# A two-layer decoder on one core: work of the opening regrouped between GpSimd, ScalarE and VectorE

## The chip, the cores and the metric

The kernel runs on one core of a Trainium2 chip. The metric is the device time of one execution in microseconds (us). A core has five engines with a queue each: TensorE (PE, matrix products; its weight loads are listed as PEld), VectorE (DVE), ScalarE (ACT), GpSimd (POOL) and SyncE (SP, which here only issues transfers). Each works through its own list in order and waits on semaphores. Transfers (DMA) can be issued by SP, ACT and POOL; an issuing engine is held for the issue, not for the transfer.

## The reference, cut to what matters

Two decoder layers over `x` of 8 batches x 256 tokens x 128 features. The opening of the kernel, which the change is in, works on the first of six residual blocks:

```python
def _L0_attn_ref(x, W_qkv, b_qkv, W_out, b_out):     # 16 heads of 8 columns
    qkv = x @ W_qkv.T + b_qkv
    q, k, v = jnp.split(qkv, 3, axis=-1)
    ...
    scores = jnp.einsum('bhqd,bhkd->bhqk', q, k) / jnp.sqrt(jnp.float32(HEAD_DIM))
    att = jax.nn.softmax(scores, axis=-1)
    out = jnp.einsum('bhqk,bhkd->bhqd', att, v)
    ...
    return out @ W_out.T + b_out
...
x = x + _L0_attn_ref(_layernorm(x, axis=-1), ...)
x = x + _L0_xattn_ref(_layernorm(x, axis=-1), ctx_1024, ...)   # needs K and V of ctx_1024
x = x + _L0_ffn_ref(_layernorm(x, axis=-1), ...)
x = x + _L1_attn_ref(_layernorm(x, axis=-1), ...)
x = x + _L1_xattn_ref(_layernorm(x, axis=-1), ctx_1024, ctx_1024, ...)
x = x + _L1_ffn_ref(_layernorm(x, axis=-1), ...)
```

## The kernel before, in words

Every engine has its list written out by hand; nothing is scheduled automatically. The first block runs batch by batch in steps `i` = -3 to 7 (`steps_of`), each with 16 places `h`, one for each head. In step `i`, PE computes the real scores of batch `i` (`scores`, line 1324) and, beside them, the scores of batch `i + 1` that are only used to find each row's maximum (`scores_for_max`, line 1333). DVE reduces these to row maxima (`row_max`, 954), ACT takes the exponentials (`exps`, 658), PE forms the weighted sums (1370). Steps -3, -2 and -1 are the opening: layer norms, projections and stacks are prepared for the first batches, and in step -1 the row maxima of batch 0 are found. Step 0 is the first full one.

How a batch gets ready for its scores: DVE takes statistics (`ln_stats`, 927 and 930), POOL turns them into a reciprocal deviation (`rstd_step_`, 511 and 513), DVE applies the norm (`ln_apply`, 938), PE transposes and projects (1272, 1280, 1284), ACT copies queries and keys to `qkf` (681). Then `split` (407 to 412) breaks the float32 values of `qkf` into three bfloat16 parts in `parts`, so that six products of parts (`TERMS`) give nearly float32 scores. It runs on DVE for batches 0 and 1 (`FIRST` keeps them off POOL) and on POOL for the others. Last, DMAs copy the parts into `stack` in the order of the six terms, six loads for the queries and six for the keys of a batch. SP issues them (`load_stack`, 470), except for the six key loads of batch 0, which POOL issues (`load_first_keys`, 533). `stack` has three slots (batch number mod 3). POOL clears each once with a memset (`clear_stack`, 504), and SP then writes rows of ones into it (`fill_stack`, 435). PE waits for a batch's stack in `wait_stacked`.

Keys and values of the context for the second block come from eight projections, `kv_project` (1296, 1298), copied by ACT (686, 688). `KV_AT` says in which step and at which place they stand, and PE waits for all of their copies before step 0. `BUSY` says at which places PE multiplies the identity with itself with no use of the result (`stay_busy`, 1265), to have something to do. `prepare_v_aug` (908, 910) are DVE memsets of the buffer for the values, two slots at a time.

Of the kernel before, what the change touches and what calls it, by code (L numbers as in the profile page):

```python
# [67 lines left out]
KV_AT = {-2: (15, 15, 15), -1: (1, 4, 7, 10, 13)}  # L68

FIRST = (0, 1, B, B + 1, B + 2)  # L70
# [15 lines left out]
BUSY = {(-3, 0): 10, (-3, 5): 2, (-3, 9): 4, (-2, 0): 2, (-2, 5): 2, (-2, 9): 3, (-1, 4): 3, (-1, 10): 3,  # L86
# [3 lines left out]
def build(nc, t):  # L90

    ctx = ExitStack()
    with ctx:
# [183 lines left out]
        def wait_stacked(eng, n):  # L277

            if n == 0:
                eng.wait_ge(first_keys, STACKED // 2)  # L280
            eng.wait_ge(stacked[n % 3], STACKED * (n // 3 + 1) - (STACKED // 2 if n % 3 == 0 else 0))
# [134 lines left out]
        def _(sp):  # L416
# [22 lines left out]
            for s3 in range(3):  # L439
                fill_stack(s3)  # L440
# [31 lines left out]
            for lo in MANY:  # L472
                for i in range(lo - 3, lo + B):
                    if has(i + 3, lo):
                        load_stack(i + 3)
                    if lo == 0:
                        load_for_later(i)
# [11 lines left out]
        def _(pool):  # L489
# [39 lines left out]
            def load_first_keys():  # L529

                pool.wait_ge(parts_ready, 1)
                for r, (jq, jk) in enumerate(TERMS):
                    pool.dma_start(stack[r::DH, 0, 1], parts[:, 0, 1, jk, :]).then_inc(first_keys, 16)
# [72 lines left out]
            for lo in MANY:  # L606
# [12 lines left out]
                for n in range(lo, lo + B):  # L619
                    if n == 0:  # L620
                        rstd_step_(0)
                        rstd_step_(1)
                        clear_stack(1)
                        clear_stack(2)
                        load_first_keys()
                    elif 2 <= n < B or n == B + AHEAD_C:
                        rstd_step_(item(n))
# [24 lines left out]
        def _(act):  # L652
# [72 lines left out]
            def v_copy_ahead(m):  # L725
# [3 lines left out]
                               pv_ps[1][:, 0, :].rearrange("p (h d) -> p h d", d=DH), ACT.Copy).then_inc(v_ready, 1)  # L729

# [60 lines left out]
            for lo in MANY:  # L791
# [33 lines left out]
                for i in steps_of(lo):  # L825
                    x = prepared(i, lo)
                    for h in range(H):
# [23 lines left out]
                        if h == 15 and x is not None and has(i + 3, lo):  # L851
                            v_copy(i + 3)
                        if h == 0 and lo == B and has(i - 3, lo):
# [50 lines left out]
        def _(dve):  # L904
# [174 lines left out]
            for lo in MANY:  # L1079
# [29 lines left out]
                for i in steps_of(lo):  # L1109
                    x = prepared(i, lo)  # L1110
                    for h in range(H):
# [4 lines left out]
                        if (lo == 0 and h == 0 or (i, h) == (B, 1)) and ln is not None and ln != 1:  # L1116
                            ln_stats(ln)
                            if ln == 0:
                                ln_stats(1)
                        if has(i + 1, lo):  # L1120
# [7 lines left out]
                        if h == 3 and i == -3:  # L1128
                            prepare_v_aug(slice(2, 4), 2)
# [5 lines left out]
                        if (i, h) == (-2, 9):  # L1135
                            split(dve, 1)
# [625 lines left out]
```

## Time and profile before

| | |
|---|---|
| time, median of 3 runs | 397.46 us (396.42 to 400.72) |
| time of the profiled execution | 399.4 us |
| its span in the trace | 397.6 us |
| PE busy | 354.7 us (89% of the span) |
| PE weight loads | 210.5 us (53%) |
| DVE busy | 314.7 us (79%) |
| ACT busy | 265.6 us (67%) |
| POOL busy | 160.4 us (40%) |
| granted PE clock, mean | 0.985 of 2.4 GHz |

A profile shows one execution. A timeline row gives start, duration, engine, line, operation and tiles, with the idle time before it and what ended it in brackets. The chain of waits leads back from the last instruction, at each step to what released it. "Granted clock" is the share of its full 2.4 GHz that PE was given in a stretch. All times in the rows are us from the start of the span.

### The profile page before, as it was taken

How to read it: one execution, taken by the hardware profiler on the slowest of the kernel's cores; microseconds unless marked ns; L12 is line 12 of the kernel's file. 1: busy time of each engine (PE TensorE's matmuls, PEld its weight loads, DVE VectorE, ACT ScalarE, POOL GpSimd, SP SyncE). 2: the span in 40 equal slices, each digit the busy share in tenths (PEclk: the TensorE clock that was granted, in tenths of full speed). 3: DMA queues.
4: the chain of work that ended last, by engine and by line, in shares of the span. 5: the costliest groups of instructions: out<-in, count | busy, mean ns of one | idle time of the engine just before them, and what ended most of it. 6: DMA issues, size and time to landing. Idle time of an engine off the chain costs nothing.

```text
span 397.6 us, 9590 instructions
## 1 busy us (share of the span) xinstructions
PE 354.7 (89%) x3246; PEld 210.5 (53%) x3246; DVE 314.7 (79%) x874; ACT 265.6 (67%) x594; POOL 160.4 (40%) x267
## 2 busy tenths in 40 slices
PE   6889999999999889987887969999889899989994
PEld 6765444444444468775266834444444444447564
DVE  7778889989998277976367667898988997479995
ACT  3436888888878757767306666887777887765751
POOL 8425653565200023445006274157677422370001
PEclk9999999999999999999899898999999999999999
DMA  7442243224330000002000311311311300000003
GB/s 221 124 109 53 77 115 81 54 51 115 91 134 2 2 0 3 0 2 66 14 2 3 80 42 40 83 43 41 81 35 49 82 2 3 2 1 2 1 2 106
DMA packets 35830, 20.00 MB, mean 50 GB/s; under 512 B 4150, under 2 KB 34790, under 8 KB 35782
## 3 DMA queue, kind: packets, MB, share of 16 engines
q1 hardware_dynamic: 34982, 17.81, 16.9%
q10 hardware_dynamic: 608, 1.18, 0.8%
q8 instruction: 27, 0.44, 0.5%
q0 software_dynamic: 192, 0.39, 0.4%
q14 instruction: 21, 0.17, 0.1%
HBM read 5.58 MB, written 1.05 MB: 17 GB/s over the span
## 4 chain that ended last, share of the span: by engine, by line
PE 64%; DVE 13%; issue 6%; ACT 6%; POOL 5%; DMA 3%; SPq 2%; ACTq 0%; POOLq 0%; DVEq 0%
PE pv_ps L1370 15%; PE s_ps L1324 14%; PE s_ps L1427 4%; DVE negmax_sb L954 3%; PE prep_ps L1280 3%; PE s_ps L1333 3%; ACT probT_sb L658 3%; PE s_ps L1663 3%; PE out_ps L1482 2%; DVE xn_sb L938 2%; PE s_ps L1450 2%; PE prep_ps L1284 2%; PE s_ps L1510 2%; PE s_ps L1500 2%; PE out_ps L1401 2%
## 5 line engine op out<-in xcount | busy, mean ns | idle before, releaser
L954 DVE TENSOR_REDUCE negmax_sb<-s_ps 128x2 bf16<-128x512 f32 x256 | 163.9, 691 | 33.9 <-PE s_ps L1333 33.2
L658 ACT ACTIVATE probT_sb<-s_ps 128x512 f32<-128x512 f32 x256 | 143.3, 596 | 32.3 <-PE s_ps L1324 29.1
L1324 PE MATMUL s_ps<-stack_sb 63*128 63x256 bf16 x512 | 89.9, 273 | 11.1 <-ACT probT_sb L658 4.7
L1333 PE MATMUL s_ps<-stack_sb 62*128 62x256 bf16 x512 | 87.1, 274 | 6.0 <-DMA stack_sb<-parts_sb 4.6
L1370 PE MATMUL pv_ps<-probT_sb,v_aug_sb 128*32 128x256 f32 x1024 | 68.8, 386 | 0.5 <-ACT probT_sb L658 0.5
L1324 PEld LDWEIGHTS s_ps<-stack_sb 63*128 63x128 bf16 x512 | 30.8, 94 | 67.3 <-ACT probT_sb L658 38.2
L511 POOL TENSOR_SCALAR rstd_sb<-mv_sb 128x2 f32<-128x2 f32 x32 | 7.2, 225 | 100.5 <-DVE mv_sb L930 100.1
L1370 PEld LDWEIGHTS pv_ps<-probT_sb,v_aug_sb 128*32 128x32 f32 x1024 | 26.8, 109 | 25.9 <-issue 13.2
L1333 PEld LDWEIGHTS s_ps<-stack_sb 62*128 62x128 bf16 x512 | 29.6, 94 | 12.2 <-DMA stack_sb<-parts_sb 5.6
L681 ACT ACTIVATE qkf_sb<-prep_ps,b_qkv_sb 128x256 f32<-128x256 f32 x56 | 23.9, 470 | 13.7 <-PE prep_ps L1284 13.7
L938 DVE TENSOR_SCALAR xn_sb<-x_all_sb,mv_sb,rstd_sb 128x128 f32<-128x128 f32 x64 | 23.9, 465 | 3.8 <-POOL rstd_sb L513 3.6
L1192 DVE SCALAR_TENSOR_TENSOR late_sb<-late_sb,level_sb,k_inv_sb 8x256 f32<-8x256 f32 x49 | 23.2, 474 | 1.8
L513 POOL TENSOR_TENSOR rstd_sb<-rstd_sb,minus_half_sb 128x2 f32<-128x2 f32 x32 | 22.9, 716 | 2.7
L1280 PE MATMUL prep_ps<-xnT_sb,w_att_sb 128*128 128x256 f32 x64 | 21.9, 425 | 0.1
L407 POOL CAST parts_sb<-qkf_sb 128x512 bf16<-128x512 f32 x14 | 8.5, 609 | 29.9 <-ACT qkf_sb L681 29.9
L1427 PE MATMUL s_ps<-xrT_sb,d_w_sb 128*128 128x512 f32 x40 | 19.5, 611 | 0.8 <-ACT late_sb L746 0.8
L521 POOL TENSOR_TENSOR x_all_sb<-x_all_sb,b_vo_sb 128x256 f32<-128x256 f32 x16 | 11.5, 728 | 18.6 <-DVE xn_sb L938 18.5
L746 ACT ACTIVATE late_sb<-s_ps,d_b_sb 128x512 f32<-128x512 f32 x20 | 13.4, 686 | 6.1 <-PE s_ps L1427 6.1
L1007 DVE SCALAR_TENSOR_TENSOR x_all_sb<-out_ps,den_inv_sb,x_all_sb 128x128 f32<-128x128 f32 x32 | 9.8, 346 | 9.1 <-PE out_ps L1482 9.0
L412 POOL TENSOR_TENSOR parts_sb<-rest_sb,parts_sb 128x512 bf16<-128x512 f32 x14 | 16.2, 1160 | 1.1
L409 POOL TENSOR_TENSOR rest_sb<-qkf_sb,parts_sb 128x512 f32<-128x512 f32 x14 | 16.2, 1156 | 1.1
L410 POOL TENSOR_TENSOR parts_sb<-qkf_sb,parts_sb 128x512 bf16<-128x512 f32 x14 | 16.2, 1157 | 0.0
(206 smaller groups left out, 648.5 us busy)
## 6 DMA issues: line engine op xcount, KB each, us to landing
stack_sb<-parts_sb SPq DMA_DIRECT2D x186, 64.0 KB, 2.1
x_all_sb<-x SPq DMA_DIRECT2D x4, 256.0 KB, 3.3
ctxT_sb<-ctxT ACTq DMA_DIRECT2D x2, 512.0 KB, 6.6
f_w_sb<-f_w SPq DMA_DIRECT2D x2, 512.0 KB, 4.3
out<-x_all_sb SPq DMA_DIRECT2D x4, 256.0 KB, 2.4
d_w_sb<-d_w SPq DMA_DIRECT2D x2, 320.0 KB, 3.6
w_att_sb<-w_att SPq DMA_DIRECT2D x2, 256.0 KB, 4.0
stack_sb<-maxrow_sb ACTq DMA_DIRECT2D x32, 4.0 KB
```

Source lines behind the costliest of these rows:

```text
L409: eng.tensor_tensor(rest[:, :, :], qkf[:, w], parts[:, u, :, 0, :], ALU.subtract).then_inc(rest_ready, 1)
L513: pool.tensor_tensor(rstd[:, u, :], rstd[:, u, :], minus_half[:, 0:NT], ALU.pow).then_inc(rstd_ready, 1)
L658: act.activation(probT[:, c % 8], s2_ps[c % 2][:, :, :], ACT.Exp, scale=DH ** -0.5).then_inc(exp_ready, 1)
L681: act.activation(qkf[:, slot(n), a, :], prep_ps[:, a, :], ACT.Identity, bias=b_qkv[:, layer(n), a:a + 1]).then_inc(qk_ready, 2 if layer(n) ...
L938: i = dve.tensor_scalar(xn[:, u, k, :], x_all[:, tiles(n).start + k, :], mv[:, u, k, 0:1], rstd[:, u, k:k + 1], ALU.subtract, ALU.mult)
L954: dve.tensor_reduce(negmax[:, n % 2, :, max_column(max_head(h))], first_bank(c)[:, :, :], axis=AX.X, op=ALU.max, negate=True).then_inc(max ...
L1192: dve.scalar_tensor_tensor(out=min_junk[:, :], in0=e_row[:, :], scalar=level[:, a:a + 1], in1=k_inv[:, :], op0=ALU.min, op1=ALU.mult, accu ...
L1280: i = pe.matmul(prep_ps[:, 0, :], w_att[:, l, 0, :], xnT[:, u, :], start=True, stop=True)
L1324: i = pe.matmul(s2_ps[c % 2][:, k, :], stack[rows, s3, 1, h // 2, k * P:(k + 1) * P], stack[rows, s3, 0, h // 2, :], start=True, stop=True)
L1333: i = pe.matmul(first_bank(c)[:, k, :], stack[rows, s3, 0, hp, k * P:(k + 1) * P], stack[rows, s3, 1, hp, :], start=True, stop=True)
L1370: i = pe.matmul(pv_ps[0][32 * j:32 * j + 32, g // 2, :], v_cols[:, k, first:first + 32], probT[:, h % 8, k, :], start=(g % 2 == 0 and k == ...
L1427: pe.matmul(up_bank(c), d_w1[:, f, :], xrT[:, 2 * S * q:2 * S * (q + 1)], start=True, stop=True).then_inc(d_h_psum, 1)
```

## The change

It changes only the order and the engine of work in steps -3 to -1:

- POOL clears slot 1 of the stack only when both first norms are applied (`xn_ready` 2), and slot 2 only behind the loads of the first keys. SP writes the ones of slot 2 in step -1.
- Of batch 0's six key loads POOL issues four and ACT two.
- The statistics of batch 2 (DVE) and the memset of the third and fourth slot for values move from ahead of the splits to behind the first; POOL takes its step for batch 2 right behind the memset of slot 2.
- The split of batch 1 moves from DVE to POOL.
- The projections of the context move: one into step -3, three spread over step -2 (which had three at its end), four in step -1 (which had five). The three groups of matmuls without use in step -2 go.

```diff
-KV_AT = {-2: (15, 15, 15), -1: (1, 4, 7, 10, 13)}
-FIRST = (0, 1, B, B + 1, B + 2)
+KV_AT = {-3: (9,), -2: (1, 6, 10), -1: (4, 7, 10, 13)}
+KEYS_BY_POOL = 4
+FIRST = (0, B, B + 1, B + 2)
-BUSY = {(-3, 0): 10, (-3, 5): 2, (-3, 9): 4, (-2, 0): 2, (-2, 5): 2, (-2, 9): 3, (-1, 4): 3, (-1, 10): 3,
+BUSY = {(-3, 0): 10, (-3, 5): 2, (-3, 9): 4, (-1, 4): 3, (-1, 10): 3,
@@ SP
-            for s3 in range(3):
+            for s3 in range(2):
                 fill_stack(s3)
...
                 for i in range(lo - 3, lo + B):
+                    if i == -1:
+                        fill_stack(2)
@@ POOL
                 pool.wait_ge(parts_ready, 1)
-                for r, (jq, jk) in enumerate(TERMS):
-                    pool.dma_start(stack[r::DH, 0, 1], parts[:, 0, 1, jk, :]).then_inc(first_keys, 16)
+                for r in range(KEYS_BY_POOL):
+                    pool.dma_start(stack[r::DH, 0, 1], parts[:, 0, 1, TERMS[r][1], :]).then_inc(first_keys, 16)
...
                         rstd_step_(0)
                         rstd_step_(1)
+                        pool.wait_ge(xn_ready, 2)
                         clear_stack(1)
+                        load_first_keys()
                         clear_stack(2)
-                        load_first_keys()
-                    elif 2 <= n < B or n == B + AHEAD_C:
+                        rstd_step_(2)
+                    elif 3 <= n < B or n == B + AHEAD_C:
@@ ACT
+            def load_first_keys():
+                act.wait_ge(parts_ready, 1)
+                for r in range(KEYS_BY_POOL, len(TERMS)):
+                    act.dma_start(stack[r::DH, 0, 1], parts[:, 0, 1, TERMS[r][1], :]).then_inc(stacked[0], 16)
...
+                        if (i, h) == (-3, 15):
+                            load_first_keys()
@@ DVE
-                        if (lo == 0 and h == 0 or (i, h) == (B, 1)) and ln is not None and ln != 1:
+                        if (lo == 0 and h == 0 or (i, h) == (B, 1)) and ln is not None and ln not in (1, 2):
...
+                        if (i, h) == (-2, 0):
+                            ln_stats(2)
+                            prepare_v_aug(slice(2, 4), 2)
...
-                        if h == 3 and i == -3:
-                            prepare_v_aug(slice(2, 4), 2)
...
-                        if (i, h) == (-2, 9):
-                            split(dve, 1)
```

`wait_stacked` is changed to the new counts (64 on `first_keys`, the rest on `stacked`).

POOL's list, from the second norm's reciprocal to the third batch's bias add. Before:

```order
L513 TENSOR_TENSOR rstd_sb<-rstd_sb,minus_half_sb 128x2 [waits rstd_step]
L504 MEMSET stack_sb 128x2048 x2
L533 DMA stack_sb<-parts_sb 16x8x256 [waits parts_ready]
L533 DMA stack_sb<-parts_sb 16x8x256 x5
L521 TENSOR_TENSOR x_all_sb<-x_all_sb,b_vo_sb 128x256 [waits xn_ready,bias_folded] x2
L511 TENSOR_SCALAR rstd_sb<-mv_sb 128x2 [waits mv_ready]
L513 TENSOR_TENSOR rstd_sb<-rstd_sb,minus_half_sb 128x2 [waits rstd_step]
L521 TENSOR_TENSOR x_all_sb<-x_all_sb,b_vo_sb 128x256 [waits xn_ready,bias_folded]
```

The same place in the changed kernel:

```order
L507 MEMSET stack_sb 128x2048 [waits xn_ready]
L536 DMA stack_sb<-parts_sb 16x8x256 [waits parts_ready]
L536 DMA stack_sb<-parts_sb 16x8x256 x3
L507 MEMSET stack_sb 128x2048
L514 TENSOR_SCALAR rstd_sb<-mv_sb 128x2 [waits mv_ready]
L516 TENSOR_TENSOR rstd_sb<-rstd_sb,minus_half_sb 128x2 [waits rstd_step]
L524 TENSOR_TENSOR x_all_sb<-x_all_sb,b_vo_sb 128x256 [waits xn_ready,bias_folded] x2
L408 CAST parts_sb<-qkf_sb 128x2x256 [waits parts_ready,qk_ready]
L410 TENSOR_TENSOR rest_sb<-qkf_sb,parts_sb 128x512 [waits part1_ready]
L411 TENSOR_TENSOR parts_sb<-qkf_sb,parts_sb 128x2x256
L413 TENSOR_TENSOR parts_sb<-rest_sb,parts_sb 128x2x256 [waits rest_ready]
```

The second memset stands behind the key loads now, and the four rows of batch 1's split stand behind both bias adds.

ACT's list from the biases of the values (`bv_cols`) to the queries and keys of batch 1 (the `qkf` rows). Before:

```order
L735 ACTIVATE bv_cols_sb<-ident_sb,b_qkv_sb 128x128
L715 ACTIVATE v_aug_sb<-prep_ps 128x32x8 [waits v_aug_ready,v_psum]
L668 ACTIVATE xnT_sb<-prep_ps 128x256 [waits xnT_psum]
L681 ACTIVATE qkf_sb<-prep_ps,b_qkv_sb 128x256 [waits qk_psum]
L681 ACTIVATE qkf_sb<-prep_ps,b_qkv_sb 128x256
```

The same place in the changed kernel:

```order
L691 ACTIVATE k_ctx_sb<-s_ps,b_qkv_sb 128x256 [waits kv_psum]
L693 ACTIVATE v_ctx_sb<-s_ps 128x256
L720 ACTIVATE v_aug_sb<-prep_ps 128x32x8 [waits v_aug_ready,v_psum]
L740 DMA stack_sb<-parts_sb 16x8x256 [waits parts_ready]
L740 DMA stack_sb<-parts_sb 16x8x256
L691 ACTIVATE k_ctx_sb<-s_ps,b_qkv_sb 128x256 [waits kv_psum]
L693 ACTIVATE v_ctx_sb<-s_ps 128x256
L673 ACTIVATE xnT_sb<-prep_ps 128x256 [waits xnT_psum]
L691 ACTIVATE k_ctx_sb<-s_ps,b_qkv_sb 128x256 [waits kv_psum]
L693 ACTIVATE v_ctx_sb<-s_ps 128x256
L686 ACTIVATE qkf_sb<-prep_ps,b_qkv_sb 128x256 [waits qk_psum]
```

Copies of three context projections and the two key loads, which wait for batch 0's parts, stand ahead of batch 1's `qkf`.

DVE's list from the last apply of the opening to the statistics of batch 2. Before:

```order
L938 TENSOR_SCALAR xn_sb<-x_all_sb,mv_sb,rstd_sb 128x128
L908 MEMSET v_aug_sb 128x2048
L910 MEMSET v_aug_sb 128x64 [waits v_aug_ready]
L407 CAST parts_sb<-qkf_sb 128x2x256 [waits qk_ready]
L409 TENSOR_TENSOR rest_sb<-qkf_sb,parts_sb 128x512 [waits part1_ready]
L410 TENSOR_TENSOR parts_sb<-qkf_sb,parts_sb 128x2x256
L412 TENSOR_TENSOR parts_sb<-rest_sb,parts_sb 128x2x256 [waits rest_ready]
```

The same place in the changed kernel:

```order
L408 CAST parts_sb<-qkf_sb 128x2x256 [waits qk_ready]
L410 TENSOR_TENSOR rest_sb<-qkf_sb,parts_sb 128x512 [waits part1_ready]
L411 TENSOR_TENSOR parts_sb<-qkf_sb,parts_sb 128x2x256
L413 TENSOR_TENSOR parts_sb<-rest_sb,parts_sb 128x2x256 [waits rest_ready]
L960 TENSOR_TENSOR b_vo_sb<-out_ps,b_vo_sb 128x128 [waits fold_psum,parts_ready]
L940 BN_STATS stats_sb<-x_all_sb 128x6 [waits x_in1]
L940 BN_STATS stats_sb<-x_all_sb 128x6
L943 BN_AGGR mv_sb<-stats_sb 128x2 [waits stats_ready] x2
L921 MEMSET v_aug_sb 128x2048
L923 MEMSET v_aug_sb 128x64 [waits v_aug_ready]
```

The memset went from ahead of batch 0's split to behind it, and no second split follows.

## Rows read from the trace of the kernel before

**Rows 1.** Chain of waits in order of time, the opening: start, duration, what.
```profile
6.49 3.61 DVE xn_sb L938 x2
...
17.97 2.59 DMA stack_sb<-parts_sb
...
33.77 0.28 PE s_ps L1324
```

**Rows 2.** Timeline of DVE, the opening: start, duration, engine, line, operation.
```profile
1.48 1.76 DVE L908 MEMSET v_aug_sb<- 128x2048 f32 x1 [0.38 <-issue]
...
12.35 0.39 DVE L407 CAST parts_sb<-qkf_sb 128x512 bf16<-128x512 f32 x1
...
14.11 0.69 DVE L412 TENSOR_TENSOR parts_sb<-rest_sb,parts_sb 128x512 bf16<-128x512 f32 x1
...
17.11 0.69 DVE L412 TENSOR_TENSOR parts_sb<-rest_sb,parts_sb 128x512 bf16<-128x512 f32 x1
...
23.31 0.60 DVE L938 TENSOR_SCALAR xn_sb<-x_all_sb,mv_sb,rstd_sb 128x128 f32<-128x128 f32 x2
```

**Rows 3.** Timeline of POOL, the opening.
```profile
2.39 1.80 POOL L504 MEMSET stack_sb<- 128x2048 f32 x1
...
6.41 3.55 POOL L504 MEMSET stack_sb<- 128x2048 f32 x2
15.11 3.39 POOL L533 DMA_DIRECT2D stack_sb<-parts_sb  x6 [5.15 <-DVE parts_sb L412]
18.51 1.42 POOL L521 TENSOR_TENSOR x_all_sb<-x_all_sb,b_vo_sb 128x256 f32<-128x256 f32 x2
...
20.20 0.72 POOL L513 TENSOR_TENSOR rstd_sb<-rstd_sb,minus_half_sb 128x2 f32<-128x2 f32 x1
...
29.39 0.61 POOL L407 CAST parts_sb<-qkf_sb 128x512 bf16<-128x512 f32 x1 [4.62 <-ACT qkf_sb L681]
...
32.43 1.15 POOL L412 TENSOR_TENSOR parts_sb<-rest_sb,parts_sb 128x512 bf16<-128x512 f32 x1
```

**Rows 4.** Timeline of ACT, the opening.
```profile
8.60 0.84 ACT L681 ACTIVATE qkf_sb<-prep_ps,b_qkv_sb 128x256 f32<-128x256 f32 x2 [1.22 <-PE prep_ps L1284]
...
16.98 0.47 ACT L686 ACTIVATE k_ctx_sb<-s_ps,b_qkv_sb 128x256 f32<-128x256 f32 x1 [1.68 <-PE s_ps L1298]
17.35 0.38 ACT L688 ACTIVATE v_ctx_sb<-s_ps 128x256 f32<-128x256 f32 x1
```

**Rows 5.** Timeline of PE: the opening, and one row further on.
```profile
11.29 0.61 PE L1307 MATMUL prep_ps<-w_att_sb,xnT_sb 128*128 128x128 f32 x4
...
15.90 0.60 PE L1296 MATMUL s_ps<-ctxT_sb,w_att_sb 128*128 128x256 f32 x2
...
16.77 0.60 PE L1296 MATMUL s_ps<-ctxT_sb,w_att_sb 128*128 128x256 f32 x2
...
20.87 0.40 PE L1333 MATMUL s_ps<-stack_sb 62*128 62x256 bf16 x4 [1.95 <-DMA stack_sb<-parts_sb]
...
190.68 0.39 PE L1333 MATMUL s_ps<-stack_sb 62*128 62x256 bf16 x4 [2.69 <-DMA stack_sb<-parts_sb]
```

**Rows 6.** Line 470 (SP): batch 0, its last two landings, batch 2 twice.
```profile
L470 SPq DMA_DIRECT2D stack_sb<-parts_sb x6: 595/604/619, 14.8 to 18.1; - x6
...
DMA to landing us min/median/max: 2.7/2.8/2.8
...
L470 SPq DMA_DIRECT2D stack_sb<-parts_sb x12: 532/598/820, 33.6 to 40.8; - x12
...
DMA to landing us min/median/max: 2.0/2.1/3.1
```

**Rows 7.** Timeline of DVE beside a split on POOL, in the middle layers.
```profile
216.03 1.43 DVE L938 TENSOR_SCALAR xn_sb<-x_all_sb,mv_sb,rstd_sb 128x128 f32<-128x128 f32 x2
```

**Rows 8.** Stretches: length; busy PE, PEld, DVE, ACT, POOL; clock; DMA share; GB/s.
```profile
20.80:24.00 3.20, 2.99 (x22) 2.02 (x22) 2.60 (x6) 0.75 (x2) 0.12 (x1) 1.00 0.36 91
...
190.00:192.00 2.00, 1.32 (x6) 0.60 (x7) 0.90 (x2) 0.00 (x0) 0.00 (x0) 0.78 0.08 22
```

More of the change, by code:

```diff
@@ L279, in wait_stacked @@
             if n == 0:
-                eng.wait_ge(first_keys, STACKED // 2)
-            eng.wait_ge(stacked[n % 3], STACKED * (n // 3 + 1) - (STACKED // 2 if n % 3 == 0 else 0))
+                eng.wait_ge(first_keys, 16 * KEYS_BY_POOL)
+            eng.wait_ge(stacked[n % 3], STACKED * (n // 3 + 1) - (16 * KEYS_BY_POOL if n % 3 == 0 else 0))
         def has(n, lo):
```

## The prediction

> **What bounds the kernel now.** I read the page first: TensorE (PE) is busy for most of the span, at the full granted clock nearly throughout, and nothing of the change touches the layers behind the opening. So the question is by how much the first full step (step 0: real scores of batch 0 with scores for the maximum of batch 1) starts earlier; whatever follows it follows at its old distance. I then read the chain of waits in order of time up to that step [rows 1]. It goes through four pieces. The second layer norm's apply on VectorE (DVE) takes 3.61 us. After it come a memset and the split of batch 0. The stack loads follow, whose last GpSimd (POOL) issue at 17.97 lands 2.59 later. Step 0 starts at 33.77. The stack of batch 0 is what PE waited 1.95 us for before 20.87 [rows 5].
>
> The timelines of the engines show why. The two pieces of the apply that wait 3.61 us run beside POOL's two stack memsets (3.55 us from 6.41) [rows 3] and end just behind them; two unhindered tensor_scalars of that form take about 0.6. The split then starts at 12.35 [rows 2], although its input was complete at 8.60 + 0.84 = 9.44 [rows 4].
>
> **The change, part by part.**
>
> *The first split.* With POOL's memset waiting for the apply, the apply ends near 7.1, POOL clears slot 1 from 7.1 to 8.9, and the DVE memset stands behind the split. The split then starts when its input is there, 9.5, and takes what it took, 12.35 to 14.81 = 2.46 [rows 2]. Batch 0's parts are ready at 11.95 instead of 14.81: 2.85 us earlier. The memset clear of slot 1 is hidden behind ScalarE's (ACT's) copies; were it 0.6 longer, it would reach the split.
>
> *The stack of batch 0.* SP issues six query loads at 14.8 to 18.07, one each 0.65, and the sixth takes 2.7 to 2.8 to land, so about 20.8; POOL's sixth key landed at 17.97 + 2.59 = 20.56 [rows 1, 6]. The two queues finish together, so taking two keys from POOL leaves SP's queries as the last to land. I cost that edit at nothing but a lighter burst: SP's sixth landing after 2.1 (its quickest) to 2.8. Batch 0's stack is there at 11.95 + 3.26 + 2.1 to 2.8 = 17.3 to 18.0.
> The Trainium skill (Kernel Development and Optimization, Key Constraints) says the same of such a split: all queues share 16 DMA engines, so another issuer saves issue time alone. By it the edit saves POOL two issues of 0.53 and no landing.
>
> *What it costs ACT.* ACT issues its two keys before its copies for batch 1. PE's eight warm-up matmuls end at 11.29, where now the first context projection stands (one each 0.87, 15.90 to 16.77), then the value projection (0.45) [rows 5]. ACT copies the projection 1.08 after its start (16.98 against 15.90), 0.75 for its two copies, 0.38 for the value copy [rows 4, 5]: 13.5. Two issues at SP's 0.60 [rows 6], or one as long as POOL's 0.77 first, end at 14.7 to 14.9. The next context copy (0.75) and the transposed batch 1 (0.35) end at 15.9; the batch 1 projections run to 17.0, their copies (0.84) to 17.9, the value projection to 18.4. So PE reaches the first scores at 18.3 to 18.9, and the loads are no longer what it waits for: 2.0 to 2.6 us gained at this place, not 2.85. The removed warm-ups lie in waits and are worth nothing. The moved projection too: behind the first scores DVE runs three row maxima without a gap, and the apply of batch 2 starts at 23.31, 2.44 after PE's 20.87 [rows 2, 5], whether PE projects in between or not.
>
> *The second split on POOL.* This is the dear part. POOL is behind: keys issued from 12.25 (0.3 after the parts), four instead of six: 0.77 + 3 x 0.525 = 2.34, to 14.6; the memset of slot 2 1.8, to 16.4; the statistics step 1.0 (from the adds' end at 18.51 + 1.42 = 19.93 to 20.20 + 0.72 = 20.92); two bias adds 1.42; 18.85. The split on POOL takes 29.39 to 33.58 = 4.19 [rows 3], against 2.47 on DVE. Batch 1's parts are ready at 23.05, where DVE had them at 17.11 + 0.69 = 17.80 [rows 2]: 5.2 us later. Its input, at 17.9, is just in time. SP then issues twelve loads; the twelfth starts 7.2 after the first and lands 2.1 later (at most 3.1) [rows 6]: batch 1's stack is there at 32.4 to 33.2. Step 0's first matmul needs it. Before it was there by 29 and hid behind everything; that cover is now gone.
>
> *The other arm to step 0.* From the first scores to step 0 passed 33.77 - 20.87 = 12.9. From 18.3 to 18.9 this gives 31.2 to 31.8. On top comes a hold: the apply of batch 2 falls at about 21.1, inside POOL's split. Where that happened before, at 216.03, two applies took 1.43 instead of the 0.60 of 23.31 [rows 2, 7]; at worst they wait for the rest of one POOL instruction of 1.15 and for the whole of the next, some 1.6 together [rows 3]. With 0 to 1.6 more this arm ends at 31.2 to 33.4.
> The Trainium skill (SBUF — State Buffer, SBUF: two separate sides) states it as an exclusive lock on a port pair of VectorE and GpSimd, held for a whole instruction; the trace agrees (3.61 us beside the two memsets).
>
> **Sum.** Step 0 starts at the later of 32.5 to 33.3 and 31.2 to 33.4: 33.77 becomes 32.5 to 33.4, a gain of 0.4 to 1.3; I take 0.85, the middle. Steps 0 and later run at PE's pace, as before; batch 2's twelve loads, at 33.6 to 40.8 before [rows 6], find SP free from 31 on and are no later than they were. The profiled execution took 399.4 us with a span of 397.6; less 0.85 that is 398.55 and 396.75. The median of the three runs is 397.46, 1.94 below that execution, so the median should be 396.6.
>
> **Rivals.**
> - *Batch 1's stack does not bind, and the gain of the first split comes through.* It needs POOL ready 1.5 us sooner, for instance by a copy step that DVE's statistics let start earlier, or SP issuing at its quickest 0.53. Then the other arm ends at 31.2: gain 2.2 to 2.6, 395.1. Against it: POOL's terms are all rows of plain operations, with no wait among them that could vanish.
> - *Slower: POOL is held while it issues the keys.* DVE's second memset (1.76) now lies at 13.2 to 15.0, beside POOL's third and fourth key. If it holds POOL for its length, POOL's list, batch 1's parts and its stack slip by up to 1.76: stack at 34.2 to 35.0, step 0 0.4 to 1.2 later than now, 398.3. It decides from 0.9 us of hold on. Against it: DVE's first memset at 1.48 to 3.24 and POOL's at 2.39 to 4.19 overlapped, and each took what it takes alone, 1.76 and 1.80 [rows 2, 3].
> The Trainium skill (SBUF — State Buffer, the box on DVE blocking DMA in SBUF: two separate sides) says a two-port DVE instruction keeps GpSimd from writing its DMA's descriptors until it ends; whether this memset is one, no row here shows.
> - *Slower: PE's clock falls.* PE now waits between the end of the row-maximum step and the stack, 1 to 2 us. After 2.69 us without work before 190.68 the granted share in 190 to 192 was 0.78, so the clock went to 1.2 GHz; after 1.95 before 20.87 it stayed at 1.00 [rows 5, 8]. Such an episode at half rate, 0.22 x 2 us lost and more beyond, costs an estimated 1.7 us where PE sets the pace: 396.6 + 1.7 = 398.3. It needs a wait of over 2 us, which the sum just misses.
> - *No change at all*, because the stack lands at 33.7: the upper end of landing times (3.1 instead of 2.1). It lies within the first case's own spread.
>
> **How the numbers follow.** The first case with its spread 0.55, the full gain 0.17, POOL held 0.13, the clock 0.12, something unseen 0.03. The range takes in the full gain and the two slower cases, 395.1 to 398.3, and about 0.4 on either side for the scatter of medians (the three runs lie between 396.42 and 400.72): 394.8 to 398.7. The likeliest case alone would be 396.1 to 397.1. A change under 1% (4 us) can't be told from none in this kernel; only a clock that falls or stays up in several further places could carry it past 1%, in either direction. So 0.03, 0.94 and 0.03.
>
> **What would show it.** In the changed profile: the second apply of the opening back near 0.6 us and the DVE split ending at about 12.0 (wrong if the POOL memset still holds it). PE's first scores at 18.3 to 18.9, with ACT's copies as what ended the wait. POOL's split of batch 1 at 18.9 to 23.1. SP's twelve loads from 23.1, and PE's wait before step 0 ended by a DMA into the stack, at 32.5 to 33.4. If that wait is ended by ACT instead, the bound was the other arm. I am wrong if step 0 starts before 31.8 or after 33.9, or if the granted share is below 1.00 between 30 and 40 us.

## The result, and the profile after

| | before | after |
|---|---|---|
| time, median | 399.45 us (20 runs, 396.42 to 401.24) | 396.76 us (20 runs, 394.18 to 401.06) |
| time of the profiled execution | 399.4 us | 399.54 us |
| its span | 397.6 us | 397.7 us |
| its granted PE clock, mean | 0.985 | 0.978 |
| PE busy | 354.7 us | 354.4 us |
| DVE busy | 314.7 us | 310.6 us |
| POOL busy | 160.4 us | 163.3 us |

The ratio is 0.9936, 95% interval 0.991 to 0.9961: 2.6 us less (about 0.6%), under the 1% that counts as a difference here. Three of the changed kernel's 20 runs (400.1 to 401.06 us) count as slow (over 1.5% above its fastest); the median has them in, and without them it is 396.43. The median is the predicted 396.6 within 0.2. The size of the gain is not: I had forecast 0.85, from a median of three runs (397.46) that lay 2 us below what 20 runs of the same kernel give. And the same changed kernel, timed later beside other runs of the kernel before, came to 0.9982 (0.9954 to 1.001), which can't be told from no change. Most of both goes with TensorE's clock, and it is the subject of the second half.

The timeline of DVE after, the opening (start, duration, engine, line, operation; in brackets the idle time before and what ended it):

```profile
6.66 0.60 DVE L951 TENSOR_SCALAR xn_sb<-x_all_sb,mv_sb,rstd_sb 128x128 f32<-128x128 f32 x2 [0.41 <-POOL rstd_sb L516]
9.56 0.43 DVE L408 CAST parts_sb<-qkf_sb 128x512 bf16<-128x512 f32 x1 [2.30 <-ACT qkf_sb L686]
...
11.35 0.69 DVE L413 TENSOR_TENSOR parts_sb<-rest_sb,parts_sb 128x512 bf16<-128x512 f32 x1
...
13.36 1.76 DVE L921 MEMSET v_aug_sb<- 128x2048 f32 x1 [0.38 <-issue]
...
20.32 1.56 DVE L951 TENSOR_SCALAR xn_sb<-x_all_sb,mv_sb,rstd_sb 128x128 f32<-128x128 f32 x2
```

The two applies are back at 0.60 from 3.61 [rows 1], the split starts when its input is there, and batch 0's parts are ready at 12.04 instead of 14.81 [rows 2]. The last row is new: the apply of batch 2 takes 1.56 where it took 0.60 [rows 2], because of what POOL does then:

```profile
7.32 1.81 POOL L507 MEMSET stack_sb<- 128x2048 f32 x1 [0.70 <-DVE xn_sb L951]
12.36 2.35 POOL L536 DMA_DIRECT2D stack_sb<-parts_sb  x4 [3.23 <-DVE parts_sb L413]
14.70 1.82 POOL L507 MEMSET stack_sb<- 128x2048 f32 x1
...
17.50 1.40 POOL L524 TENSOR_TENSOR x_all_sb<-x_all_sb,b_vo_sb 128x256 f32<-128x256 f32 x2
18.86 0.60 POOL L408 CAST parts_sb<-qkf_sb 128x512 bf16<-128x512 f32 x1
...
21.88 1.15 POOL L413 TENSOR_TENSOR parts_sb<-rest_sb,parts_sb 128x512 bf16<-128x512 f32 x1
```

The memset of slot 1 stands behind the applies, the four key issues take 2.35 beside DVE's memset, and the split of batch 1 runs from 18.86 to 23.03. Line 471 on SP, the loads of batch 0's queries, then of all of batch 1 (duration ns least, median, most; first and last start; time to landing):

```profile
L471 SPq DMA_DIRECT2D stack_sb<-parts_sb x6: 598/605/622, 12.1 to 15.3; - x6
...
DMA to landing us min/median/max: 2.1/2.4/3.0
...
L471 SPq DMA_DIRECT2D stack_sb<-parts_sb x12: 532/598/600, 23.1 to 30.0; - x12
```

PE after:

```profile
18.09 0.61 PE L1345 MATMUL s_ps<-stack_sb 62*128 62x256 bf16 x6
...
22.03 0.60 PE L1284 MATMUL prep_ps<-ident_sb,xn_sb 128*128 128x128 f32 x2 [1.18 <-DVE xn_sb L951]
22.43 1.08 PE L1308 MATMUL s_ps<-ctxT_sb,w_att_sb 128*128 128x256 f32 x2
...
33.86 0.27 PE L1336 MATMUL s_ps<-stack_sb 63*128 63x256 bf16 x1 [0.67 <-ACT v_ctx_sb L693]
```

The first scores start at 18.09 instead of 20.87 and wait for no load any more [rows 5]. But step 0 starts at 33.86, where it was at 33.77 [rows 1]: 2.78 us were won at the first scores, and all of it was gone 15.8 us later. The projection at 22.43 takes 1.08 where the same form took 0.60 [rows 5]; that is PE at the half clock. The stretches of after (columns as in [rows 8]; the clock is the last but two):

```profile
18.00:22.00 4.00, 2.27 (x18) 1.27 (x17) 3.48 (x6) 0.56 (x2) 3.84 (x6) 1.00 0.00 0
22.00:26.00 4.00, 3.97 (x17) 2.96 (x18) 2.15 (x4) 1.13 (x3) 1.75 (x2) 0.57 0.21 53
26.00:30.00 4.00, 3.94 (x28) 2.94 (x27) 2.72 (x5) 1.48 (x4) 0.96 (x2) 1.00 0.39 98
```

PE is busy for 2.27 of the 4 us from 18 to 22, while it waits for row maxima (0.57) and for the held apply (1.18), and then has 1.2 GHz from 22.1 to 25.5. The kernel before had 1.00 throughout the opening, 20.80 to 24.00 among it [rows 8].

A second execution of the same changed kernel shows the other side. PE's start of step 0, its DVE apply, and two stretches:

```profile
33.03 0.27 PE L1336 MATMUL s_ps<-stack_sb 63*128 63x256 bf16 x1 [1.34 <-DVE negmax_sb L967]
```

```profile
20.38 1.59 DVE L951 TENSOR_SCALAR xn_sb<-x_all_sb,mv_sb,rstd_sb 128x128 f32<-128x128 f32 x2
```

```profile
30.00:34.00 4.00, 2.66 (x22) 1.51 (x20) 3.46 (x9) 1.58 (x4) 2.29 (x4) 1.00 0.50 138
34.00:40.00 6.00, 6.00 (x52) 2.98 (x48) 4.09 (x8) 3.44 (x8) 0.94 (x2) 0.72 0.42 108
```

The apply is held as much, yet the clock stays up and step 0 starts at 33.03, as the prediction had it (32.5 to 33.4). The last of batch 1's twelve loads lands at 32.83. The row names DVE (`negmax_sb`) as what ended the 1.34 us of waiting, but the last row maxima of this step had ended at 32.42, 0.6 before; the load is what came just before. PE did 2.66 us of work in these 4 us, and the half clock came from 35.0 to 38.5. Before this run I had expected step 0 at 32.2 to 32.9 and a ratio of 0.991 to 0.996; both were missed (33.03, 0.9982).

### The profile page after: what moved, and what is told of

It is laid out like the page before. It is cut to its first block, busy times and chain, and to the rows that moved or that the text cites. A ratio compares the mean times of both kernels' runs of the same rounds, so it can differ in the third digit from the quotient of the medians.

```text
span 397.7 us, 9561 instructions
## 1 busy us (share of the span) xinstructions
PE 354.4 (89%) x3232; PEld 209.3 (53%) x3232; DVE 310.6 (78%) x870; ACT 265.8 (67%) x594; POOL 163.3 (41%) x269
## 4 chain that ended last, share of the span: by engine, by line
PE 66%; DVE 12%; ACT 6%; issue 6%; POOL 4%; DMA 3%; SPq 2%; ACTq 1%; POOLq 0%; DVEq 0%
PE pv_ps L1382 15%; PE s_ps L1336 14%; DVE negmax_sb L967 4%; PE s_ps L1439 4%; PE prep_ps L1292 3%; PE s_ps L1345 3%; PE s_ps L1675 3%; ACT probT_sb L663 3%; PE out_ps L1494 2%; PE s_ps L1462 2%; PE prep_ps L1296 2%; PE s_ps L1522 2%; PE prep_ps L1319 2%; PE out_ps L1413 2%; SPq L471 2%
## 5 line engine op out<-in xcount | busy, mean ns | idle before, releaser
L1345 PE MATMUL s_ps<-stack_sb 62*128 62x256 bf16 x512 | 88.5, 278 | 4.7 <-DMA stack_sb<-parts_sb 2.7
L1382 PE MATMUL pv_ps<-probT_sb,v_aug_sb 128*32 128x256 f32 x1024 | 70.0, 392 | 0.5 <-ACT probT_sb L663 0.5
L951 DVE TENSOR_SCALAR xn_sb<-x_all_sb,mv_sb,rstd_sb 128x128 f32<-128x128 f32 x64 | 21.3, 374 | 3.6 <-POOL rstd_sb L516 3.6
L413 POOL TENSOR_TENSOR parts_sb<-rest_sb,parts_sb 128x512 bf16<-128x512 f32 x15 | 17.4, 1159 | 1.2
L410 POOL TENSOR_TENSOR rest_sb<-qkf_sb,parts_sb 128x512 f32<-128x512 f32 x15 | 17.3, 1155 | 1.2
L411 POOL TENSOR_TENSOR parts_sb<-qkf_sb,parts_sb 128x512 bf16<-128x512 f32 x15 | 17.4, 1157 | 0.0
```

The costliest lines, as they stand in the source:

```text
L411: eng.tensor_tensor(parts[:, u, :, 1, :], qkf[:, w], parts[:, u, :, 0, :], ALU.subtract).then_inc(rest_ready, 1)
L951: i = dve.tensor_scalar(xn[:, u, k, :], x_all[:, tiles(n).start + k, :], mv[:, u, k, 0:1], rstd[:, u, k:k + 1], ALU.subtract, ALU.mult)
L1345: i = pe.matmul(first_bank(c)[:, k, :], stack[rows, s3, 0, hp, k * P:(k + 1) * P], stack[rows, s3, 1, hp, :], start=True, stop=True)
L1382: i = pe.matmul(pv_ps[0][32 * j:32 * j + 32, g // 2, :], v_cols[:, k, first:first + 32], probT[:, h % 8, k, :], start=(g % 2 == 0 and k == ...
```

## The clock: why executions of one kernel differ

Each run has its mean granted clock beside its time. The kernel before, 35 runs beside the last four experiments, by that clock (median of each group, number of runs):

| mean clock | before | the wait alone (three comparisons) | changed kernel (first comparison; second) |
|---|---|---|---|
| 0.994 | | 394.8 (2), 395.4 (5), 395.3 (3) | 394.7 (4) |
| 0.989 to 0.990 | 398.2 to 398.4 (16) | 396.3 to 396.6 (8) | 396.4 (4) |
| 0.985 to 0.986 | 399.5 to 399.6 (9) | 397.5 to 398.3 (10) | 397.3, 398.1 (6); 398.5, 398.7 (6) |
| 0.981 | 400.9 (10) | | 400.1 (1); 400.2 (3) |

The clock moves in steps, and from step to step the same program takes 1.3 to 1.4 us more. One stretch at half clock like the one from 22.1 to 25.5 above is one such step: 3.4 x 0.5 / 397 = 0.0043 of the mean. So a kernel's median is its time at equal clock plus 1.3 to 1.4 us for each such stretch that an execution has, and the number of them differs from one execution to the next, in the middle layers above all (190 to 250 us: 0.89 to 0.95 in the profiles). The changed kernel's spread of 394 to 401 us is this. I fitted one slope to all runs (314 us per 1.00 of clock) and give "at equal clock" below: the mean time moved along it to 0.985, less the same for the kernel before. Its error is 0.1 to 0.3 us, several times less than that of a median. It leaves out what a kernel's edit itself does to the clock, so the medians stand beside it.

## The experiments

| kernel | median, runs | ratio to before (95%) | mean clock | at equal clock, us |
|---|---|---|---|---|
| changed kernel | 396.76, 20 | 0.9936 (0.991, 0.9961) | 0.987 | -1.7 |
| changed kernel again | 398.71, 12 | 0.9982 (0.9954, 1.001) | 0.985 | -1.1 |
| memset_only: the wait alone | 395.47, 6 | 0.9895 (0.9864, 0.9926) | 0.991 | -1.9 |
| memset_only_2: same | 395.96, 12 | 0.9939 (0.991, 0.9968) | 0.990 | -1.6 |
| wait_alone_3: same | 396.62, 12 | 0.9939 (0.9914, 0.9964) | 0.989 | -1.8 |
| split1_dve | 399.55, 12 | 0.9994 (0.9972, 1.0016) | 0.982 | -1.2 |
| keys_pool | 399.78, 12 | 1.0001 (0.9965, 1.0036) | 0.980 | -1.5 |
| both | 398.73, 12 | 0.9979 (0.9956, 1.0003) | 0.983 | -1.6 |
| busy_back | 399.1, 12 | 1.0012 (0.9985, 1.0039) | 0.984 | -0.5 |
| best | 398.86, 12 | 0.998 (0.9953, 1.0007) | 0.987 | -0.4 |
| wait_pool_split | 399.44, 12 | 1.0002 (0.9975, 1.0028) | 0.986 | +0.1 |
| wait_no_warmups | 397.2, 12 | 0.9932 (0.9909, 0.9955) | 0.988 | -1.9 |
| wait_kv_at | 398.56, 12 | 0.9989 (0.9963, 1.0015) | 0.984 | -1.4 |

The medians of before in the three comparisons of the experiments were 399.35 (29 runs), 399.56 (35) and 399.46 (35), its mean clock 0.986 in each. Each comparison ran on another chip, so kernels of different comparisons are compared only through the kernel before: memset_only, split1_dve, keys_pool and both in the first; the changed kernel again, memset_only_2, busy_back and best in the second; the others in the third. The first row's last number is taken against the first of these three, in which the changed kernel itself did not run.

### The wait alone

To the kernel before, one line:

```diff
                         rstd_step_(1)
+                        pool.wait_ge(xn_ready, 2)
                         clear_stack(1)
```

> The kernel before with one line more: GpSimd waits for both norms' applies before it clears slot 1. If the memsets beside the apply were what held the first split, the apply takes 0.6 us instead of 3.6, the DVE memset ends at about 9.3 and the split of batch 0 at about 12.0 (14.8 before); PE's first scores come when its three context projections are done, at 18.9 (20.9 before), and step 0 starts near 31.9: 1.9 us less than before, ratio 0.995. The rival, that the gain of the changed kernel comes from the regrouped key loads and projections, expects under 0.5 us.

Measured: 395.47 us, 0.9895. POOL, DVE and PE of its first profile:

```profile
7.10 3.55 POOL L504 MEMSET stack_sb<- 128x2048 f32 x2 [0.70 <-DVE xn_sb L939]
```

```profile
6.44 0.60 DVE L939 TENSOR_SCALAR xn_sb<-x_all_sb,mv_sb,rstd_sb 128x128 f32<-128x128 f32 x2 [0.41 <-POOL rstd_sb L513]
7.42 1.76 DVE L909 MEMSET v_aug_sb<- 128x2048 f32 x1 [0.37 <-issue]
...
9.65 1.28 DVE L407 CAST parts_sb<-qkf_sb 128x512 bf16<-128x512 f32 x1 [0.23 <-ACT qkf_sb L682]
```

```profile
32.22 0.28 PE L1325 MATMUL s_ps<-stack_sb 63*128 63x256 bf16 x1
```

The applies are free. POOL's two memsets now lie beside DVE's own memset, which isn't slowed (1.76), and reach into the split, whose first cast waits for their end (1.28 instead of 0.39 [rows 2]; 1.64 in the two repetitions). The parts are ready at 12.98, 1.83 earlier than before, PE's first scores come at 19.02, 1.85 earlier, step 0 at 32.22, 1.55 earlier, and the clock is 1.00 up to 188.7. So nearly all of the first gain reaches step 0. Twice repeated:

> memset_only once more beside its rivals on one chip. If its gain is 1.55 us of earlier step 0 and the rest clock: at equal granted clock 1.8 us under before, ratio 0.990 to 0.995. If the first result was luck of six executions, 0.996.

> The kernel before with POOL's wait for the two applies ahead of its first stack memset, timed a third time as the base of this comparison. Its two runs so far gave 0.9895 and 0.9939 of the time before. Theory (the memsets held the applies, and 1.5 us of the opening go): 0.990 to 0.996, step 0 at 32.2 to 32.4, granted clock 1.00 until then. Rival (what it gained was that the clock fell less often in those executions): a ratio of 0.997 or more, with a mean clock no higher than that of the kernel before.

Measured 0.9939 both times, step 0 at 32.27 and 32.07, no fall of the clock ahead of it in any of the three profiles. The theory held: 1.6 to 1.9 us at equal clock, and the rest of what the medians show (2.8 to 3.9) goes with the clock, whose mean was 0.989 to 0.991 instead of 0.986. In the comparison in which the changed kernel had 398.71, this had 395.96.

### Parts of the change taken back

From the changed kernel: batch 1's split on DVE again (split1_dve), all six keys on POOL again (keys_pool), and the two together (both).

```diff
-FIRST = (0, B, B + 1, B + 2)
+FIRST = (0, 1, B, B + 1, B + 2)
...
                             fold_bias(0)
+                        if (i, h) == (-2, 9):
+                            split(dve, 1)
```

```diff
-KEYS_BY_POOL = 4
+KEYS_BY_POOL = 6
```

> The changed kernel with batch 1's split back on DVE. If GpSimd's split costs by holding the apply of batch 2 and by the late stack of batch 1, the apply takes 0.6 instead of 1.56 us and batch 1's stack is there by 29. But the input of this split is complete at 17.4 only, so it ends at 19.9 and the row maxima start 1.4 us later than in the changed kernel (18.5): together 0 to 0.5 us slower than the changed kernel, ratio to before 0.994 to 0.996. If the split's place were indifferent: as the changed kernel.

> The changed kernel with all six first keys issued by GpSimd, none by ScalarE. If SP's six queries end last anyway (17.56 in the changed kernel), the first stack is there at 17.6 to 17.9 and PE's first scores stay near 18.1. GpSimd's split of batch 1 ends 1.05 us later (24.1) and its stack lands near 33.1 instead of 32.1. Step 0 then starts 0 to 1 us later than in the changed kernel: ratio to before 0.994 to 0.997. If the second queue is what gave the gain: PE's first scores 1 us later, ratio 0.996 or more.

> The changed kernel with both taken back: keys by GpSimd alone and batch 1's split on DVE. ScalarE is free 1.3 us sooner, the input of batch 1's split is complete near 16.1, the split ends near 18.6 as the first scores arrive, the apply of batch 2 isn't held. Step 0 starts near 31.2 with no wait for batch 1's stack: 0.5 to 1.5 us faster than the changed kernel, ratio to before 0.990 to 0.993. If the two edits are what made the changed kernel faster: 0.996 or more.

Measured: 0.9994, 1.0001, 0.9979. All three lie outside what I had expected, and "both", which was to be the fastest (0.990 to 0.993), most of all. Taking parts back did not recover a gain. For "both" PE and DVE show why:

```profile
21.11 0.60 PE L1347 MATMUL s_ps<-stack_sb 62*128 62x256 bf16 x2 [2.50 <-DVE negmax_sb L967]
```

```profile
16.88 0.88 DVE L408 CAST parts_sb<-qkf_sb 128x512 bf16<-128x512 f32 x1 [1.60 <-ACT qkf_sb L686]
...
20.36 1.90 DVE L967 TENSOR_REDUCE negmax_sb<-s_ps 128x2 bf16<-128x512 f32 x3
```

DVE's split of batch 1 starts at 16.88 (15.33 before: its end at 17.80 less 2.47 [rows 2]), since its input `qkf` comes later from ACT. It now lies ahead of the row maxima, PE waits 2.50 us for them, and the clock is halved from 20.5 to 27.3. Step 0 comes at 35.13. In split1_dve this wait is 2.93. So the split on POOL keeps DVE free for the row maxima once ACT is late. The times don't show a use of it: "both" and keys_pool, timed side by side, differ by this split alone and came to -1.6 and -1.5 at equal clock. The two keys on ACT are another matter: with all six on POOL the first scores start at 17.94, 0.15 earlier than at 18.09, so the edit gains nothing there, as predicted. (They wait for a load again there, for 0.33 us, where the changed kernel waits for none.) keys_pool's profile has the half clock from 21.1 to 27.9 and step 0 at 34.73, its runs a mean clock of 0.980 but -1.5 at equal clock: at equal clock nothing sets it apart from the changed kernel (-1.7 and -1.1).

### The warm-up matmuls put back

```diff
-        ... (-3, 9): 4, (-1, 4): 3, ...
+        ... (-3, 9): 4, (-2, 0): 2, (-2, 5): 2, (-2, 9): 3, (-1, 4): 3, ...
```

> The changed kernel with the seven warm-up matmuls of step -2 put back. The changed kernel's profile shows half clock from 22.3 to 25.7, behind PE's pauses between 18.7 and 22.0. If it is the removed warm-ups that let it fall: granted share 1.00 through 20 to 30, step 0 about 1 us earlier than 33.86, mean clock up by 0.004 and time down by 1.4 us against the changed kernel, ratio 0.990. If the pauses behind the held apply do it: the clock falls as often as in the changed kernel and the time is the same within 0.5 us or longer, as the warm-ups delay the first scores.

Measured: 1.0012, no gain; at equal clock -0.5, where the changed kernel beside it had -1.1. PE and DVE:

```profile
23.03 0.41 PE L1284 MATMUL prep_ps<-ident_sb,xn_sb 128*128 128x128 f32 x2 [1.99 <-DVE xn_sb L951]
```

```profile
20.51 2.37 DVE L951 TENSOR_SCALAR xn_sb<-x_all_sb,mv_sb,rstd_sb 128x128 f32<-128x128 f32 x2
```

The clock was halved from 23.6 to 27.0 all the same, behind a pause of 1.99 us that comes from the held apply. The hold itself was 2.37 - 0.60 = 1.77 us, a little over my bound of 1.6. The other direction, from the wait alone:

> The wait for the applies, and the three groups of warm-up matmuls of step -2 (7 matmuls) taken out. Theory (they lie in waits, and the clock falls behind pauses, of which these 7 shorten none behind the first scores): as with the wait alone within 0.4 us, clock 1.00 until step 0. Rival (without them PE does too little ahead of the first scores, and the clock falls in the opening): a stretch at half clock between 15 and 30 us of the span, 1.4 us or more slower, 397 to 398.

Measured: 0.9932, beside 0.9939 for the wait alone in the same comparison; step 0 at 32.80, 0.7 later, of which a mean clock of 0.83 from 10 to 20 us accounts. At equal clock it is -1.9 against -1.8, by the means 0.2 us slower, by the medians 0.6. The theory that it costs nothing held at equal clock; the rival was seen in the trace (the clock did fall in the opening once, from 15 to 18.4).

### What gives the gain back

Each with the wait for the applies; only batch 1's split to POOL, and only the projections' places (with the warm-ups of step -2 out):

```diff
-FIRST = (0, 1, B, B + 1, B + 2)
+FIRST = (0, B, B + 1, B + 2)
...
-                        if (i, h) == (-2, 9):
-                            split(dve, 1)
```

```diff
-KV_AT = {-2: (15, 15, 15), -1: (1, 4, 7, 10, 13)}
+KV_AT = {-3: (9,), -2: (1, 6, 10), -1: (4, 7, 10, 13)}
```

> The wait for the applies, and of the change's other parts only the split of batch 1 on POOL. Theory (this split is what gives the gain back): POOL issues six keys from about 13.3 to 16.7, then adds and the step of batch 2 (2.4) to 19.1, the split 4.2 to 23.3; the twelve loads 7.2 and a landing of 2.1 to 3.1: stack of batch 1 at 32.6 to 33.6, step 0 0.4 to 1.4 later than with the wait alone (32.22), the apply of batch 2 held to 1.5 us or more, and PE waiting over 1 us behind it, with a fall of the clock in part of the executions: 396.5 to 397.5, ratio 0.993 to 0.998. Rival (the split alone is hidden, and the late step 0 of the changed kernel comes from its projections and statistics moved): as with the wait alone, 395.5 to 396, step 0 at 32.2 to 32.4.

> The wait for the applies, with the changed kernel's places of the projections (one in step -3, three spread over step -2, four in step -1) and without the warm-ups of step -2. Theory (one projection fewer in step -1 lies beside waits for row maxima, worth nothing): as with the wait alone within 0.4 us, step 0 at 32.0 to 32.4. Rival 1 (PE's work was part of the bound in step -1): up to 0.9 us earlier, 31.3 to 31.8. Rival 2 (ACT's copies of projections now stand ahead of batch 1's queries and keys and make its split late): step 0 at 32.8 or later, or first scores later than 19.4.

Measured: the split on POOL takes 0.9939 back to 1.0002, 2.8 us by the medians and 1.9 at equal clock, more than I had expected (0.993 to 0.998, step 0 later by 0.4 to 1.4). POOL, DVE, PE and the stretch:

```profile
21.40 1.16 POOL L412 TENSOR_TENSOR parts_sb<-rest_sb,parts_sb 128x512 bf16<-128x512 f32 x1
22.64 0.23 POOL L511 TENSOR_SCALAR rstd_sb<-mv_sb 128x2 f32<-128x2 f32 x1
22.95 0.72 POOL L513 TENSOR_TENSOR rstd_sb<-rstd_sb,minus_half_sb 128x2 f32<-128x2 f32 x1
```

```profile
23.71 0.60 DVE L939 TENSOR_SCALAR xn_sb<-x_all_sb,mv_sb,rstd_sb 128x128 f32<-128x128 f32 x2 [1.77 <-POOL rstd_sb L513]
```

```profile
24.45 0.66 PE L1271 MATMUL prep_ps<-ident_sb,xn_sb 128*128 128x128 f32 x2 [2.07 <-DVE xn_sb L939]
...
35.66 0.28 PE L1323 MATMUL s_ps<-stack_sb 63*128 63x256 bf16 x1
```

```profile
22.00:28.00 6.00, 3.93 (x18) 2.75 (x18) 2.40 (x5) 1.13 (x3) 2.22 (x4) 0.72 0.30 76
```

Here the split is ahead of batch 2's statistics step on POOL, so the apply doesn't run held but starts only at 23.71 and PE waits 2.07 us. Step 0 comes at 35.66, 3.6 later than with the wait alone (32.07). Batch 1's stack, by which I had worked out the expectation, had landed at 31.64 and doesn't bind. The changed kernel avoids the worst of this with its third part, statistics and POOL's step of batch 2 ahead of the split: there the apply starts at 20.32, though held. So the parts of the change hang together: the split on POOL costs the whole gain when the step for batch 2 stands behind it.

The projections' places: 0.9989, 1.4 us at equal clock instead of 1.8, and 1.9 us by the medians. Against the wait without the warm-ups, which differs from it by the places alone, these are 0.6 and 1.4 us. Step 0 comes at 35.67, 3.6 later than with the wait alone in these two executions. Rival 2 of its expectation is what the rows show:

```profile
19.23 0.59 PE L1334 MATMUL s_ps<-stack_sb 62*128 62x256 bf16 x6 [1.67 <-DMA stack_sb<-parts_sb]
21.71 0.60 PE L1334 MATMUL s_ps<-stack_sb 62*128 62x256 bf16 x2 [1.88 <-DVE negmax_sb L955]
```

```profile
20.00:28.00 8.00, 6.29 (x25) 4.28 (x26) 5.30 (x14) 1.13 (x3) 1.67 (x3) 0.57 0.30 75
```

ACT copies the projections ahead of batch 1's `qkf`, which DVE gets at 16.83 instead of 15.09, its split ends at 20.33 and holds the row maxima; PE has fewer projections to do in its waits. With the wait alone the stretch 20 to 28 was:

```profile
20.00:28.00 8.00, 7.75 (x56) 5.62 (x56) 6.71 (x13) 3.35 (x9) 1.46 (x3) 1.00 0.38 97
```

### An attempt at a better one

The wait, slot 2 cleared only behind the keys, its ones written in step -1, and one projection in step -3:

```diff
-KV_AT = {-2: (15, 15, 15), ...
+KV_AT = {-3: (9,), -2: (15, 15), ...
...
+                        pool.wait_ge(xn_ready, 2)
                         clear_stack(1)
-                        clear_stack(2)
                         load_first_keys()
+                        clear_stack(2)
```

> The kernel before, with GpSimd waiting for both norms' applies before it clears slot 1, slot 2 cleared behind the first keys, and one of the three context projections of step -2 moved into step -3; keys and both splits stay where they were. If the first split and PE's own list bound the first scores, they come near 18.0 instead of 19.0 in memset_only, step 0 starts near 31.2 (33.77 before, 32.22 in memset_only), and PE has no long pause in step -1, so its clock stays at 2.4 GHz there: 2.2 to 2.8 us less than before at equal clock, ratio 0.988 to 0.992. Rival: ScalarE's last maxrow load or copies bind and nothing is gained over memset_only (ratio 0.990, step 0 at 32.2).

Measured: 0.998, step 0 at 33.67: a miss. The clock was 1.00 here up to 191.8. The memset taken from ahead of the first split now lies beside the second one's cast, and the bias adds beside what follows:

```profile
16.42 1.37 DVE L407 CAST parts_sb<-qkf_sb 128x512 bf16<-128x512 f32 x1 [4.12 <-ACT qkf_sb L684]
17.83 1.09 DVE L409 TENSOR_TENSOR rest_sb<-qkf_sb,parts_sb 128x512 f32<-128x512 f32 x1
18.84 1.21 DVE L410 TENSOR_TENSOR parts_sb<-qkf_sb,parts_sb 128x512 bf16<-128x512 f32 x1
```

```profile
22.15 0.39 PE L1336 MATMUL s_ps<-stack_sb 62*128 62x256 bf16 x2 [1.52 <-DVE negmax_sb L957]
```

Batch 1's split takes 4.4 us instead of the 2.5 of the kernel before, and the row maxima are late. But the kernel to hold it against is the wait alone (memset_only), and there the split is held too:

```profile
15.50 0.43 DVE L407 CAST parts_sb<-qkf_sb 128x512 bf16<-128x512 f32 x1 [2.19 <-ACT qkf_sb L682]
15.96 1.10 DVE L409 TENSOR_TENSOR rest_sb<-qkf_sb,parts_sb 128x512 f32<-128x512 f32 x1
16.98 1.21 DVE L410 TENSOR_TENSOR parts_sb<-qkf_sb,parts_sb 128x512 bf16<-128x512 f32 x1
```

It runs from 15.50 to 19.33, 3.8 us. So of the 1.45 us by which the row maxima start later in "best" (21.43 against 19.98), the split's length is 0.5 and its start 0.9: `qkf` comes later from ACT, since PE has the moved projection at 11.31 and gets to batch 1's projections at 14.38 instead of 13.46. A kernel with the memset moved and the projection left in place was not run. The wait alone, with or without the warm-ups, stays the fastest kernel of the study.

## Why the prediction was right, and where it was not

- *The first split*: right. Parts at 12.04, forecast 11.95; nothing of the memset reached it.
- *The stack of batch 0*: right. SP's sixth load landed at 17.56 (17.3 to 18.0), as the last one; ACT's two keys landed at 15.59 and 16.46, so the edit was worth nothing for the landing, and keys_pool confirms it.
- *What it costs ACT*: right in kind, 0.2 us off. PE's first scores came at 18.09 instead of 18.3 to 18.9, with no wait ahead of them, neither for a load nor for ACT. ACT's queue issued at 12.91 and 13.59 partly beside its own copy of 13.10, where I had put all in a row.
- *The second split on POOL*: right to 0.02 us in its end (23.03), and SP's loads followed at once. The stack landed at 32.11 and 32.83 in the two executions (32.4 to 33.2 forecast; the terms add up to 33.35 at the upper end), and bound step 0 in the one whose clock stayed up.
- *The hold of batch 2's apply*: 0.96 and 0.99 us, within the 0 to 1.6; busy_back showed 1.77. I counted it as delay of DVE alone. What I missed is that PE waits meanwhile and may lose its clock.
- *Step 0*: forecast 32.5 to 33.4; 33.03 in one execution, 33.86 in the other, there ended by ACT's copy of the last projection, as a late "other arm" behind a stretch of half clock and a maximum-row load that took ACT 1.40 us to issue (1.10 in the other execution).
- *Rival, POOL held while it issues keys*: refuted; four issues took 2.35 beside DVE's memset, as forecast (2.34), and six took 3.39 both without it [rows 3] and beside it (keys_pool).
- *Rival, the full gain*: step 0 at 31.2 was seen in no profile, with any kernel.
- *Rival, the clock*: this is the step that failed. I put the pause before step 0 and said that it needs over 2 us. It came 11 us earlier, behind waits of 0.57 and 1.18, and in the second execution behind 1.34 before step 0. There the share in 34 to 40 was 0.72, and a share below 1.00 between 30 and 40 was one of my own signs of being wrong. I had its price at 1.7; a stretch costs 1.3 to 1.4.
- *The moved projections at nothing*: wrong. wait_kv_at gives 0.4 to 0.6 us at equal clock and 1.4 to 1.9 by the medians. I looked at whether PE would be late, not at ACT's copies, which stand ahead of batch 1's `qkf`, nor at what PE then lacks to do while it waits.
- *The warm-ups at nothing*: right beside the wait alone (0.1 us at equal clock). Put back into the changed kernel they cost 0.6 at equal clock; in neither are they worth anything.
- *The sum*: 0.85 forecast. At equal clock it is 1.1 to 1.7, by the ratios 0.7 and 2.6. That the forecast of the median was met is luck, two errors that cancel: the base of three runs was 2 us low, and the gain in that comparison 1.8 us larger. Why the changed kernel gains more at equal clock in whole runs than the 0.74 that its best profile shows at step 0, and why its two comparisons differ by 0.6, stays open; each has profiles of a single execution only.

## What to carry to other kernels

Look for GpSimd work that merely comes early, a memset above all, beside VectorE operations on the critical path: one wait that orders it behind them gave here at least what a change of five parts was worth (-1.6 to -1.9 against -1.1 to -1.7 us at equal clock). Before moving work off an engine, list what stands behind it on the new engine (here the statistics step of the next batch) and who is held beside it. Where the clock gate decides medians, compare at equal granted clock, and look at PE's pauses as a cost of their own, even where nothing waits for PE's next result.

## What the runs showed of the hardware

- *VectorE and GpSimd*: two applies took 3.61 us beside two back-to-back memsets [rows 1, 3] and 0.60 without; a cast up to 1.64 instead of 0.39 to 0.43; an apply 1.56 to 2.37 beside a split. VectorE's memset (1.76) and its row maxima, which read PSUM (1.89 for three beside POOL's split, 1.90 in "both", where POOL has no split then), weren't held. So it goes by the operation, not by the engine being busy. The Trainium skill (SBUF — State Buffer, SBUF: two separate sides) names the conditions: operations in a two-port mode, or with two SBUF inputs against a GpSimd operation that reads SBUF. The split's subtractions agree: 1.09 to 1.22 beside POOL's bias adds, 0.69 alone. Of the two applies in the kernel before, the first alone, a single instruction, took 3.55 us beside two memsets of 1.80, so it did not get its turn between them:

```profile
6.49 3.55 DVE L938 TENSOR_SCALAR xn_sb<-x_all_sb,mv_sb,rstd_sb 128x128 f32<-128x128 f32 x1 [0.41 <-POOL rstd_sb L513]
```

- *The clock*: between 18 and 30 us it fell in all four profiles in which PE's longest wait there was 1.99 to 2.93 us (busy_back, wait_pool_split, both, split1_dve), in three of the six with 1.18 to 1.95 (1.18 in the changed kernel, 1.19 in keys_pool, 1.88 in wait_kv_at; not behind 1.95 in the kernel before, 1.52 in "best" and 1.20 in the changed kernel's second execution), and in none of the three of the wait alone, with 0.69 at most. In wait_no_warmups it fell earlier, behind 0.93. So a pause makes a fall likelier, but one profile doesn't tell whether a kernel has it; the mean clock of a dozen runs does. The Trainium skill (TensorE: Matmul & The Clock Gate, Part 1) describes the gate's observation as running freely, not bound to the kernel's start, which fits executions of one program that differ.
- *Issues*: ACT's first maximum-row load took 1.08 to 1.40 us to issue and the next ones 0.50 to 0.54, in all fourteen profiles; it lies just ahead of step 0.
